# Experts of a gated block: order of the next expert's weight splits, of the token takes and of the closing products

## The reference

```python
x = x + tanh(g_xattn[0]) * xattn(layernorm(x), ctx_512, ctx_512)
x = x + tanh(g_ffn[0]) * ffn(layernorm(x), w_cls, bias, w_gate_up, w_down)

# ffn: 4096 tokens of 1024, softmax over 64 logits, 8 picked for a token;
# 32 of the 64 are experts, each takes at most CAP = 512 tokens
gu = einsum('ech,ehf->ecf', buf, w_gate_up)      # 1024 -> 2 x 512
g, u = split(gu, 2, axis=-1)
act = silu(g) * u
y = einsum('eci,eih->ech', act, w_down)          # 512 -> 1024
```

## Time and profile before

| | |
|---|---|
| median of three runs | 2343.86 us (2340.87 to 2344.35) |
| the profiled execution | 2340.87 us, its span 2339.1 us |
| mean granted clock of TensorE | 0.951 of full speed |
| busy in the span: TensorE, VectorE, ScalarE, GpSimd | 89%, 62%, 52%, 44% |
| expert stage: the first gate and up product starts | 872.05 us |
| experts with one block: their gate and up products start | 1324.46, 1454.65, 1686.50, 1818.46, 2064.87, 2229.28, 2259.16 us |

### The profile page before, as it was taken

How to read it: one execution, slowest core, us unless ns; L and a number is a source line. 1 busy time by engine, 2 the same in 40 slices (tenths; PEclk the granted TensorE clock), 3 DMA queues, 4 the chain that set the end, 5 groups by cost and what they waited for, 6 DMA issues and landing times. The chain is left out here.

```text
span 2339.1 us, 43844 instructions
## 1 busy us (share of the span) xinstructions
PE 2076.8 (89%) x14528; PEld 1215.4 (52%) x14529; DVE 1460.9 (62%) x2432; ACT 1215.5 (52%) x1798; POOL 1025.8 (44%) x1224
## 2 busy tenths in 40 slices
PE   4999998998999429999999899899989899989977
PEld 2455454545554214456556565644746666454454
DVE  4789889989987623346545654734555766444373
ACT  3787677767776403235444554633544655343363
POOL 2127888887887660124224341421432542130152
PEclk7999999999999759999999999999999999999988
DMA  5478676766665734567778694975694997775673
GB/s 133 114 200 181 150 196 156 172 152 177 170 138 134 199 88 146 146 161 184 190 185 202 148 265 127 244 202 145 171 244 112 235 256 178 212 182 166 148 165 91
DMA packets 557528, 401.42 MB, mean 172 GB/s; under 512 B 211030, under 2 KB 478422, under 8 KB 557456
## 3 DMA queue, kind: packets, MB, share of 16 engines
q1 hardware_dynamic: 512400, 328.45, 52.4%
q0 software_dynamic: 45056, 72.09, 14.6%
HBM read 310.94 MB, written 101.06 MB: 176 GB/s over the span
## 5 line engine op out<-in xcount | busy, mean ns | idle before, releaser
L1455 PE MATMUL psum<-xgt,wgu 128*128 128x256 f16 (+3 forms) x6144 | 861.3, 304 | 31.6 <-DVE wgu L1145 21.4
L1455 PEld LDWEIGHTS psum<-xgt,wgu 128*128 128x128 f16 x6144 | 553.3, 99 | 338.0 <-DVE wgu L1145 23.1
L718 POOL TENSOR_TENSOR spare<-spare 128x1 f32<-128x1 f32 x160 | 106.7, 667 | 952.6 <-PE psum L1464 460.9
L1464 PE MATMUL psum<-wdn,apair 128*128 128x512 f16 x1944 | 458.1, 387 | 50.6 <-ACT ys L923 40.1
L1007 DVE TENSOR_REDUCE mx<-psum 128x2 f32<-128x512 f32 x512 | 328.0, 684 | 71.4 <-PE psum L1314 68.8
L1223 DVE COPY xgt<-psum 128x1024 f16<-128x1024 f16 x256 | 168.0, 688 | 303.6 <-PE psum L1440 275.9
L923 ACT ACTIVATE ys<-psum,slots 128x512 f32<-128x512 f32 x256 | 162.7, 689 | 318.2 <-PE psum L1464 315.5
L1233 DVE SCALAR_TENSOR_TENSOR a<-psum,sg 128x512 f32<-128x512 f32 x128 | 88.2, 689 | 383.9 <-PE psum L1455 383.9
L1464 PEld LDWEIGHTS psum<-wdn,apair 128*128 128x128 f16 x1944 | 186.6, 99 | 254.2 <-issue 56.7
L667 POOL DMA_INDIRECT lists<-entry,dest x256 | 265.7, 1038 | 106.8 <-issue 70.3
L1145 DVE SCALAR_TENSOR_TENSOR wgu<-wraw,wgu 128x1024 f16<-128x1024 f32 x256 | 311.6, 1218 | 0.0
(11 more groups left out here) (148 smaller groups left out, 1944.9 us busy)
## 6 DMA issues: line engine op xcount, KB each, us to landing
wraw<-in_L_ffn_w_gate_up_dram SPq DMA_DIRECT2D x256, 512.0 KB, 6.9
wraw<-in_L_ffn_w_down_dram SPq DMA_DIRECT2D x128, 512.0 KB, 6.6
x<-in_x_dram SPq DMA_DIRECT2D x16, 1024.0 KB
qs<-qh SPq DMA_DIRECT2D x256, 64.0 KB
xr<-in_x_dram SPq DMA_DIRECT2D x16, 1024.0 KB
out_dram<-x SPq DMA_DIRECT2D x16, 1024.0 KB
pairs<-xs SPq DMA_DIRECT2D x16, 1024.0 KB, 5.8
qs<-ql SPq DMA_DIRECT2D x128, 64.0 KB
```

What stands on the lines that cost most here:

```text
L1455: mm = pe.matmul(ps_gu[:, s, h, 0:nt * P], w[:, a, k, :], xgt[:, c, k, 0:nt * P], start=(k == 0 and (a, c) == (0, 0)), stop=(k == KB - 1 a ...
L1464: mm = pe.matmul(psum[:, Y_BANK[i] + n2, :], apair[:, o, k, c * P:(c + 1) * P], w[:, a, k, :], start=(k == 0 and (a, o) == (0, 0)), stop=( ...
```

## The change

Three orders change; no instruction is added or left out.

- ScalarE: for `j` = 0, 1 as before. For `j` = 2, 3 there is one half of the next expert's block 0 between `silu` and `act_hi`. The halves of its block 1 are split after the second and the fourth `y_out`.
- VectorE: for `j` = 2, 3 only `gate_up` and `act_lo`; then both halves of the next expert's block 0; then the takes, with the halves of block 1 after the second and the sixth of them.
- TensorE: in `closing` the transposes 2 and 3 stand behind the four down products instead of between them.

```diff
@@ ScalarE, step2
-                for j in range(FB):
+                for j in range(2):
                     silu(e, j)
-                    for h in range(2):
-                        if h == 1:
-                            act_hi(e, j)
-                        if j < 2:
-                            gu_hi(e, j + 2, h)
-                        elif not last:
-                            gu_hi(e + 1, j - 2, h)
-                    if j < 2:
-                        dn_hi(e, j)
+                    gu_hi(e, j + 2, 0)
+                    act_hi(e, j)
+                    gu_hi(e, j + 2, 1)
+                    dn_hi(e, j)
+                for j in range(2, FB):
+                    silu(e, j)
+                    if not last:
+                        gu_hi(e + 1, 0, j - 2)
+                    act_hi(e, j)
                 act.wait_ge(slots_in[par], 8 * e + 16 if par == 0 else 8 * (e + 1))
                 for i in range(CT):
                     for n2 in range(2):
                         y_out(e, par, i, n2)
+                    if i < 2 and not last:
+                        gu_hi(e + 1, 1, i)
@@ VectorE, step2
-                for j in range(FB):
+                for j in range(2):
                     gate_up(e, j)
-                    for h in range(2):
-                        if h == 1:
-                            act_lo(e, j)
-                        if j < 2:
-                            gu_lo(e, j + 2, h)
-                        elif not last:
-                            gu_lo(e + 1, j - 2, h)
-                    if j < 2:
-                        dn_lo(e, j)
-                if not last:
+                    gu_lo(e, j + 2, 0)
+                    act_lo(e, j)
+                    gu_lo(e, j + 2, 1)
+                    dn_lo(e, j)
+                for j in range(2, FB):
+                    gate_up(e, j)
+                    act_lo(e, j)
+                if not last:
+                    for h in range(2):
+                        gu_lo(e + 1, 0, h)
                     for u in range(8):
                         take_t(e + 1, u)
+                        if u in (1, 5):
+                            gu_lo(e + 1, 1, u // 4)
@@ TensorE, closing
                 for k in range(FB):
                     pe.wait_ge(alo_ready, FB * e + k + 1)
                     mm = down_part(0, 0, k)
-                    if not last and k < 2:
-                        t_rows(e + 1, 2 + k)
                 mm.then_inc(y_full, 1)
+                if not last:
+                    for u in (2, 3):
+                        t_rows(e + 1, u)
```

## The result

The changed kernel takes 2360.98 us (median of four runs, 2360.73 to 2363.04) against 2343.87 us (four runs, 2340.87 to 2344.35): a ratio of 1.008, interval 1.0064 to 1.0096. It is slower by 17 us, and the forecast of 2345.0 us (2338 to 2352) was wrong. The profiled execution took 2360.78 us, its span 2359.0 us, 19.9 us more than the span of before.

A forecast was written before the change was run, and what follows sets the result against it. TensorE, busy 89% of the span, was taken as the bound, so only its waits could give. The median 2343.86 us plus 1.1 us for delayed takes, other terms nothing, gave 2345.0 us, range 2338 to 2352.

The forecast's parts named there:

- so a new order costs and gives nothing: TensorE's `closing`: transposes 3 and 4 move behind the products; block and product take 1.10 us without gap, so no difference.
- the prediction's own signs of being wrong: Landing earlier or later than 22.8 us after the first gather, or a TensorE wait not in the earlier list.
- The landing holds the first `y_out`: One-block experts: `y_out` on ScalarE waits for the previous expert's scatter-add to land, so ScalarE's reorder is worth nothing.
- Rival (a): ScalarE's queue held the first `y_out`, which would start 3.0 us earlier seven times: 21 us less, 2323 us; chance 0.09.
- The split on the take path: VectorE, before four-block experts: a split between takes six and seven delays the eighth by 0.14 us, eight times: +1.1 us.
- Rival (d): VectorE: the moved split lies wholly on the take path, +9.8 us, 2353.7 us; chance 0.03.
- (b): The moved weight loads delay the landing of the scatter-adds, 1.8 us seven times: +13 us, 2357 us; chance 0.05.
- (c): GpSimd is held by VectorE's moved split, 1.22 us seven times: 8.5 us more, 2353.5 us; chance 0.03.
- The clock: TensorE's low clock after the 5.7 us gaps: difference put at nothing, up to 5 us either way.
- Slower by over 0.2%: Whole kernel slower by more than 4.7 us: chance 0.16, of which 0.05 within the forecast.

The follow-up runs named there:

- run 1: Kernel before with only TensorE's new order in `closing` (transposes 2 and 3 behind the four products): 2363.28 us, ratio 1.0077.
- run 9: Kernel before, unchanged, run for its trace on the third chip: 2340.32 us in one run.
- run 2: Kernel before with only ScalarE's and VectorE's new orders, TensorE's order as before: 2344.72 us, ratio 1.0005.
- run 7: Kernel before with GpSimd's four scatter-adds ahead of its four gathers: 2340.83 us, ratio 0.9789 on the second chip.
- run 12: Kernel before with each of the two `closing` transposes one product later (product, product, transpose, product, transpose, product): 2343.13 us, ratio 1.0005.
- run 6: Kernel before with TensorE's order of the change and a branch tree that asks for four blocks first: 2418.88 us in a single run, second chip.
- run 3: Kernel before with `closing` as three products, transposes 2 and 3, then the last product: 2355.9 us, ratio 1.0051.
- run 5: Kernel before with `closing` as three products, transpose 2, last product, transpose 3: 2402.23 us, ratio 1.0044 on the second chip.
- run 11: Kernel before with adds first, ScalarE's new order, and VectorE's first two takes ahead of the next block 0's splits: 2320.33 us, ratio 0.9914.
- run 8: Kernel before with scatter-adds ahead of gathers plus ScalarE's and VectorE's new orders, TensorE's order as before: 2340.31 us, ratio 0.9782, second chip.

## Why the prediction was wrong

**The step that failed** is the one on TensorE: "so a new order costs and gives nothing". It priced the matmuls from a row of two kinds of work without a gap between them, and looked only at the instructions that move. It left out what stands behind them. The order changes which instructions are the last ahead of a branch, and the way from one expert's body to the next (loop end, count, branch), 1.62 to 1.99 us, is free only as long as the instructions handed out ahead of it hold more than that. In the change they hold 1.30 us. The row that could have warned was there: the reading of the count had to lie somewhere in the unbroken rows of matmuls, so it was hidden, and by what was not asked. Of the prediction's own signs of being wrong, this one came: waits of TensorE that are not in the earlier trace rows, the 16 new ones for "issue". Size of the missed term: 19.7 us by run 1 alone (2363.28 - 2343.62). In the changed kernel's trace 12.6 us of it lie at the 24 experts with more than one block, all gap but the 0.14 of the takes. Of the 7.0 us at the seven one-block experts 1.5 are the gap, behind three of them, 0.9 longer waits for `ys` and 0.5 the longer gap before the last expert; the rest isn't resolved: these experts differ by up to 1.6 us between two executions of the same kernel (run 9 and before), with the low clock behind their wait.

**The landing holds the first `y_out`**: right for this kernel. SyncE and ScalarE start together as in the earlier trace rows, ScalarE's idle time grew to 3 us each, and the waits of TensorE stayed. Rival (a) is wrong: run 2 has nothing of its gain of 21 us. What the prediction did not say is how close the second limit was: 0.49 us in the earlier trace rows meant that with an earlier landing the old order of ScalarE would hold `y_out` at the same point (run 7). The reorder is a precondition of a gain, not a gain.

**The split on the take path**: right, 8 times 0.14 us, 9.0 to 10.1 us. Rival (d), 9.8 us more, is wrong by that.

**The moved weights and GpSimd** (b, c): the landing came 22.8 us after the first gather within 0.4 in six of seven cases, and 23.94 in one. Neither rival is needed, since run 2 is within 0.15% of before.

**The clock**: the difference was put at nothing with 5 us either way. That is about the size of the unresolved part, which no run takes apart.

**Slower by over 0.2%** had a chance of 0.16, of which 0.11 lay in the rivals (b), (c) and (d), which did not happen, and 0.05 inside the forecast's range. The prediction had no rival on TensorE's own issue, and its range had none of this cost in it.

## What to carry to other kernels

Before moving work on an engine that branches or reads a register, ask what it executes while its sequencer does that; keep long instructions ahead of the branch, not many short ones, and if short ones must be late, leave one long piece between and behind them (run 12). A gap that is called "issue" and comes at the same place of every pass is a reason to look at the sequencer's own records, which name the loop's end, the read of the count and each comparison. When a wait has two candidates within half a microsecond, removing one of them gains nothing until the other is moved too, and the limit may then turn up at a third place: here it took GpSimd's order, ScalarE's order and VectorE's first takes together to gain 22 us, where each step short of that gained 0 to 4 (against before on the first or third chip).

## What the runs showed of the hardware

- From the end of the loop over a read of the count to one of four bodies, TensorE's sequencer takes 1.62 to 1.71 us (one block), 1.77 to 1.89 (two or three) and 1.90 to 1.99 (four), in the changed kernel and run 1; at the change shown, 0.60 us of 1.78 are the loop's end. Its records put a comparison that goes on without a jump at 0.07 to 0.09 us and one that jumps at 0.21 to 0.23. In run 6 one comparison more cost about 0.14 us, and one comparison and one jump less saved 0.26 to 0.3.
- What covers it is counted in instructions, weight loads among them: 33 had been handed out and not started at each of these places in the changed kernel and runs 1, 3, 5 and 12. The 36 of the fit also counts those under way. No other kernel was measured for it.
- A wait of 2.67 us left the granted clock at 1.00, the 2.4 GHz level (run 11), and one of 2.61 us with two more idle times of 1.58 and 1.49 us around it was followed by 0.50, the 1.2 GHz level, for 6 us (run 8). The wait removed was worth twice its length there; over the seven one-block experts, 12.0 us of such waits went, and they took 22.0 us less than in run 8, on another chip.
- On one chip most one- and two-block experts took 2.7 to 5.4 us longer with the gathers ahead of the adds, and not with the adds first; VectorE's first `gate_up` started up to 4.7 us after its `silu` there. The cause is open.
